# Graph layer with a gathered table: four chunks of edges gathered first as rows of x, all others from the finished table of x W1 and x

## The reference, cut to what matters

```python
theta = x[dst] - x[src]
w = sigmoid(relu(theta @ W1 + b1) @ W2 + b2)
agg = segment_sum(w * theta, dst)
indeg = segment_sum(ones, dst)
y = x + agg + indeg * (x @ W4 + b4)
out = layernorm(y)
```

## Time and profile before

| what | value |
|---|---|
| median of three runs | 4256.39 us |
| the profiled execution | 4260.33 us |
| its span (first to last instruction) | 4258.5 us |
| POOL busy | 3057.1 us (72%) |
| DVE busy | 2904.2 us (68%) |
| PE busy | 1996.0 us (47%), mean granted clock 0.654 |
| ACT busy | 1228.4 us (29%) |
| DMA | 698.18 MB, mean 164 GB/s |

### The profile page before, as it was taken

One profiled execution on the slowest core, in us unless ns is written; L12 is line 12 of the kernel. 1 busy time (PEld: TensorE's weight loads), 2 busy tenths in 40 slices (PEclk: granted clock), 3 DMA queues, 4 the chain that ended last, 5 costly groups with the idle time before them and its releaser, 6 DMA issues.

```text
span 4258.5 us, 43192 instructions
## 1 busy us (share of the span) xinstructions
PE 1996.0 (47%) x10963; PEld 1843.3 (43%) x10963; DVE 2904.2 (68%) x4875; ACT 1228.4 (29%) x2163; POOL 3057.1 (72%) x3229
## 2 busy tenths in 40 slices
PE   3544644444444444444444444444444444444444
PEld 3444644444443444444444444444444444444444
DVE  2332778767777777777777777777777777777777
ACT  2222432322232323322233222232222222222232
POOL 6333677777777777777777777777777777777776
PEclk8776766665666666666666666566666666566666
DMA  5444565555555555555555555555555555555554
GB/s 166 119 125 111 164 177 165 167 172 172 170 168 168 168 168 168 169 169 168 169 169 168 168 168 168 169 169 168 170 171 168 176 165 174 170 169 171 168 168 116
DMA packets 320392, 698.18 MB, mean 164 GB/s; under 512 B 126510, under 2 KB 202496, under 8 KB 305397
## 3 DMA queue, kind: packets, MB, share of 16 engines
q0 software_dynamic: 151344, 408.89, 34.5%
q1 hardware_dynamic: 151920, 262.96, 20.1%
q10 hardware_dynamic: 16879, 23.55, 1.9%
HBM read 663.32 MB, written 31.81 MB: 163 GB/s over the span
## 4 chain that ended last, share of the span: by engine, by line
POOL 63%; issue 21%; PE 5%; DVE 3%; ACTq 3%; DMA 2%; ACT 2%; SPq 1%; POOLq 0%; DVEq 0%
POOL arena L511 63%; ACTq L375 3%; PE ps_z L527 2%; DMA arena<-table,src_at 2%; PE ps_sum L544 1%; SPq L375 1%; DVE scaled_x L691 1%; ACT away L586 1%; ACT hot_ne L594 1%; DVE diff L670 1%; PE ps_z L522 1%; DVE ps_z L661 1%; PE ps_hid L382 1%; DVE logit L678 0%; PE ps_hid L405 0%
## 5 line engine op out<-in xcount | busy, mean ns | idle before, releaser
L511 POOL DMA_INDIRECT arena<-table,src_at x3013 | 2854.9, 948 | 930.8 <-issue 912.7
L544 PE MATMUL ps_sum<-scaled_x,hot_en 128*128 128x130 f32 x6446 | 1395.4, 401 | 1225.7 <-DVE scaled_x L691 1196.1
L544 PEld LDWEIGHTS ps_sum<-scaled_x,hot_en 128*128 128x128 f32 x6446 | 1307.3, 307 | 1289.2 <-issue 1288.3
L661 DVE TENSOR_TENSOR ps_z<-ps_z,arena 128x896 f32<-128x896 f32 x431 | 472.7, 1097 | 906.8 <-DMA arena<-table,src_at 897.6
L601 ACT ACTIVATE ps_log<-logit,b_col 128x7 f32<-128x7 f32 x461 | 124.1, 269 | 2631.5 <-DVE logit L678 2620.1
L691 DVE TENSOR_TENSOR scaled_x<-arena,ps_log 128x896 f32<-128x896 f32 x461 | 496.6, 1077 | 140.1 <-ACT ps_log L601 140.1
L670 DVE SCALAR_TENSOR_TENSOR diff<-ps_z,w_rows 128x896 f32<-128x896 f32 x461 | 502.6, 1090 | 97.2 <-PE ps_z L527 82.4
L678 DVE TENSOR_REDUCE logit<-diff 128x7 f32<-128x896 f32 x461 | 498.1, 1080 | 24.9 <-issue 1.0
L586 ACT ACTIVATE away<-dst_rows,neg_ids 126x896 bf16<-126x896 int32 x461 | 474.3, 1029 | 132.9 <-issue 127.1
L551 PE MATMUL ps_win<-w,winT 128*128 128x256 f32 x232 | 132.4, 671 | 810.8 <-DVE hot_en L683 786.9
L683 DVE TENSOR_TENSOR hot_en<-ps_win,rel 128x896 f32<-128x896 f32 x461 | 497.6, 1079 | 0.0
(11 more groups left out here) (76 smaller groups left out, 824.4 us busy)
## 6 DMA issues: line engine op xcount, KB each, us to landing
dst_rows<-in_dst SPq DMA_DIRECT2D x115, 1764.0 KB
arena<-table,src_at POOLq DMA_INDIRECT x3013
parts<-parts_of SPq DMA_DIRECT2D x461, 31.5 KB
table<-group_rows ACTq DMA_DIRECT2D x25, 500.0 KB
parts_of<-stage SPq DMA_DIRECT2D x116, 96.0 KB, 2.1
winT<-in_x_cols SPq DMA_DIRECT2D x116, 64.0 KB
window<-in_x SPq DMA_DIRECT2D x116, 64.0 KB
out<-yout SPq DMA_DIRECT2D x116, 64.0 KB
```

Source lines behind the costliest of these rows:

```text
L511: nc.gpsimd.indirect_dma_start(gath[:, slot_of(g) + t, :], None, table, ids)\
L544: last = nc.tensor.matmul(ps_sum[:, 0:SW], hot_en[:, b, t, :], scaled_x[:, b, t, :], start=(g == 0 and t == 0), stop=(stop and t == tiles_ ...
L661: v.tensor_tensor(ps_z[b][:, 0:n, :], ps_z[b][:, 0:n, :], gath[:, lo:lo + n, 0:F], ALU.subtract).then_inc(z_read, 1)
```

## The change

POOL now gathers four whole chunks first: chunks 23, 46, 69 and 92 (`z.held`), as rows of x into their own buffer `held_x` (112 gathers). It then waits for the table, for x's half of it and for the checks of the layout, and gathers all other 457 batches (3111 tiles) from the table, in a ring of the same six batches. HEAD and the path of L527 (minus_xT) are gone.

The table is made first, before any batch is computed: the 25 groups run one after the other with five PSUM places. The x half of the table is no longer stored with x W1: SP copies it from x to the table, HBM to HBM, in four transfers of 3125 rows (`copy_x`). ACT loads only the transposed columns and stores only the x W1 half (125 x 4 pieces of 512 bytes per group).

The x W1 of the held chunks (`held_u`) is computed during the 92 batches before each of them, two tiles in four steps on PE and ACT. `dst_rows` is now loaded per batch, by ACT, into three buffers. `diff` has one buffer instead of two. The checks of the layout run at the start.

```diff
-HEAD = 30
+DR = 3
+HC = 4
+STEPS = 4
+BANKS = 5
...
+        self.held = [(h + 1) * self.chunks // (HC + 1) for h in range(HC)]
...
-        dst_rows = sb("dst_rows", [P, 2, CHUNK], I32)
+        held_x = sb("held_x", [P, HC * K, F])
+        held_u = sb("held_u", [P, K, F])
+        held_xT = sb("held_xT", [P, 2, P])
+        dst_rows = sb("dst_rows", [P, DR, BATCH], I32)
...
+        held_chunk = {c: h for h, c in enumerate(z.held)}
+        ringed = [g for g in range(all_batches) if chunk_of(g) not in held_chunk]
...
+            eng.wait_ge(x_copied, 16 * HC)
...
-        def load_group(eng, k):
+        def load_group(act, k):
             s = k % STAGES
-            eng.dma_start(group_rows[0:z.tp, s, :, F:2 * F], in_table(x, k)).then_inc(group_in[s], 16)
-            eng.dma_start(group_cols[:, s, :, :], x_turned[:, k * GT:(k + 1) * GT, :]).then_inc(group_in[s], 16)
+            act.dma_start(group_cols[:, s, :, :], x_turned[:, k * GT:(k + 1) * GT, :]).then_inc(group_in[s], 16)
...
         def copy_group(act, k):
...
+            s = k % STAGES
+            act.wait_ge(turned, k + 1)
+            wait(act, table_out[s], 16 * (k // STAGES))
+            act.sem_inc(act_gate, 1)
+            if k + STAGES < z.groups:
+                load_group(act, k + STAGES)
+            nc.scalar.copy(group_u[0:z.tp, s, :, :], ps_group[k % BANKS][0:z.tp, :, :]).then_inc(turn_copied, 1)
+            act.wait_ge(turn_copied, k + 1)
+            act.dma_start(in_table(table, k)[:, :, 0:F], group_u[0:z.tp, s, :, :]).then_inc(table_out[s], 16)
+
+        def copy_x(sp):
+            each = z.nodes // HC
+            for n in range(HC):
+                sp.dma_start(table[n * each:(n + 1) * each, F:2 * F], x[n * each:(n + 1) * each, :])\
+                    .then_inc(x_copied, 16)
...
         def windows_gpsimd(pool):
...
+            for h, c in enumerate(z.held):
+                if h < 2:
+                    pool.wait_ge(src_in[h], 16 * (h + 1))
+                    pool.sem_inc(pool_gate, 1)
+                for t in range(K):
+                    ids = bass.IndirectOffsetOnAxis(ap=src_at[:, c * K + t:c * K + t + 1], axis=0)
+                    nc.gpsimd.indirect_dma_start(held_x[:, h * K + t, :], None, x, ids).then_inc(held_in[h], 16)
+            wait_for_table(pool)
+            pool.wait_ge(judged, 1)
+            pool.sem_inc(pool_gate, 1)
+            for n, g in enumerate(ringed):
+                if n >= RB:
+                    pool.wait_ge(scaled, ringed[n - RB] + 1)
...
+                if held_step(g):
+                    h, q, step_no = held_step(g)
+                    if step_no == 0:
+                        turn_held(pe, h, q)
+                    if step_no == 2:
+                        project_held(pe, h, q)
```

More of the change, by code:

```diff
@@ L66, in __init__ @@
         self.groups = self.each // GT
-        assert self.groups + 3 <= HEAD < self.batches
+        self.held = [(h + 1) * self.chunks // (HC + 1) for h in range(HC)]
+        assert self.held[0] * NB > K // 2 * STEPS + NB and self.groups > 16
 class Chain:
@@ L394, in copy_group @@
[L394 to L407, removed]
@@ new lines, in turn_held, with copy_heldT @@
+        def turn_held(pe, h, q):
+            pe.wait_ge(held_in[h], 16 * K)
+            pe.wait_ge(turn_copied, z.groups)
+            wait(pe, held_u_copied, h * (K // 2) + q)
+            for t in range(2):
+                last = nc.tensor.transpose(ps_hid[:, t * P:(t + 1) * P], held_x[:, h * K + 2 * q + t, :], ident[:, :])
+            last.then_inc(heldT_ready, 1)
+        def copy_heldT(act, h, q):
+            act.wait_ge(heldT_ready, h * (K // 2) + q + 1)
+            wait(act, held_u_ready, h * (K // 2) + q)
+            nc.scalar.copy(held_xT[:, :, :], ps_hid[:, 0:2 * P].rearrange("p (t e) -> p t e", e=P))\
+                .then_inc(heldT_copied, 1)
@@ new lines, in project_held, with copy_held @@
+        def project_held(pe, h, q):
+            pe.wait_ge(heldT_copied, h * (K // 2) + q + 1)
+            for t in range(2):
+                last = nc.tensor.matmul(ps_hid[:, (2 + t) * P:(3 + t) * P], held_xT[:, t, :], w14[:, 0:F],
+                                        start=True, stop=True)
+            last.then_inc(held_u_ready, 1)
+        def copy_held(act, h, q):
+            act.wait_ge(held_u_ready, h * (K // 2) + q + 1)
+            if h:
+                act.wait_ge(z_read, (z.held[h - 1] + 1) * NB)
+            nc.scalar.copy(held_u[:, 2 * q:2 * q + 2, :], ps_hid[:, 2 * P:4 * P].rearrange("p (t f) -> p t f", f=F))\
+                .then_inc(held_u_copied, 1)
@@ L470, in windows_sync @@
             load_window(sp, 0)
-            load_dst_rows(sp, 0)
-            for k in range(STAGES):
-                load_group(sp, k)
+            copy_x(sp)
             store_parts(sp, 0)
@@ L506, in windows_gpsimd @@
                     ids = bass.IndirectOffsetOnAxis(ap=src_at[:, g * BT + t:g * BT + t + 1], axis=0)
[L507 to L512, removed]
+                    nc.gpsimd.indirect_dma_start(gath[:, slot_of(g) + t, :], None, table, ids)\
+                        .then_inc(gathered[place[g] % RB], 16)
         def windows_tensor(pe):
@@ L613, in mid @@
                 nc.scalar.copy(stage[:, c % 2, 1, :], rest[:, :]).then_inc(mid_ready, 1)
-            high(0)
-            mid(0)
+            for k in range(STAGES):
+                load_group(act, k)
+            for g in range(DR):
+                load_dst_rows(g)
+            for k in range(z.groups):
+                copy_group(act, k)
+                if k == z.groups // 2 + 3:
+                    high(0)
+                if k == z.groups // 2 + 6:
+                    mid(0)
             act.wait_ge(const_in, 16 * 8)
@@ L773, in windows_vector @@
             place_bases(dve)
+            place_rel(dve)
+            select_carry(1)
+            for piece in range(len(JUDGE)):
+                judge(piece)
             dve.wait_ge(const_in, 16 * 8)
```

175 lines of the change are left out of this document (76 added, 99 removed).

## The result

The changed kernel takes 4104.28 us in the median of four runs (4103.46 to 4105.2), against 4257.17 us before (4256.27 to 4260.78): a ratio of 0.9639, 95% interval 0.9623 to 0.9656. That is 3.6% faster; the forecast was 4126 us and 3.1%. The profiled execution has a span of 4103.4 us.

What follows compares the result with a forecast made beforehand. The prediction took POOL, full with gathers from the table, as the bound: first such gather at 212 us + 3111 gathers x 1.252 us (3894.9) + tail 21.1 = 4128 us span, forecast median 4126 us, range 4064 to 4200.

Steps and rivals of the forecast that it cites:

- The bound: Gathers from the table: POOL never waits there, it is simply full.
- period: Time per gather from the table in steady state: kept at 1.252 us, 3111 gathers making 3894.9 us.
- The consumers: Held chunks: consumers take 6.3 to 7.7 us per batch, POOL gathers 3 to 3.5 batches ahead, the six-batch ring suffices.
- Five engines for 3125 rows: Copy of x: engines used are the largest divisor of the row count up to 16, so five of sixteen.
- T0: Start of the first gather from the table: 212 us, from 3.72 MB on each of five engines at 18.6 GB/s.
- rival 2: Copy of x: HBM to HBM pieces cost double, T0 281 us, time 4195 us; chance 14%.
- The floor of T0: Held gathers before the table: 112 x 1.25 us plus 2 x 3 us for held-up gathers, at least 150 us.
- Rival 1: Copy of x is spread or hidden, POOL and ACT set T0 at 150 to 165 us, 4064 to 4079 us; chance 20%.
- The tail: Work behind the last gather: kept at 21.1 us, since its work is the same.
- Sum: Whole span: 212 + 3894.9 + 21.1 = 4128 us.

Runs made afterwards that it cites:

- copy16: The changed kernel with the copy of x in four transfers of 3120 rows and one of 20, over sixteen engines: 4070.07 us, ratio 0.9567 to the kernel before.
- store16: The changed kernel with each group's store split into 112 and 13 partitions, the copy of x still on five engines: 4069.77 us, ratio 0.9565.
- held5: The changed kernel with five held chunks instead of four, the copy of x kept at four transfers: 4067.59 us, ratio 0.9559.
- ring5_again: The changed kernel with a ring of five batches instead of six, repeated on an ordinary chip: 4105.88 us, ratio 0.9643.
- best_third: The changed kernel with five held chunks, stores of 112 and 13 partitions and the bases in PSUM, on an ordinary chip: 4062.35 us, ratio 0.9543.
- held2: The changed kernel with two held chunks instead of four, on a slow chip: 5619.12 us, ratio 0.9954 to the kernel before there.

## Why the prediction was right, and where it was off

- **The bound.** POOL full in steady state, period 1.252: measured 1.2524 after the change. Right. That POOL's gap alone counts was shown three ways (copy16, store16, held5), each worth the 33 us or a little more.
- **The consumers.** The forecast had 3 to 3.5 batches gathered in a held chunk and six in the ring. Measured 27.3 us, 3.1 batches, and ring5_again shows that five suffice. Right. The lag was worked off after some 13 batches of the ring, not 20.
- **Five engines for 3125 rows.** Taken from the counts of three other row numbers, and exact for this one. The Trainium skill's rule (DMA: Bandwidth & Descriptors, on why a DMA increments its semaphore by 16) agrees with 3125, 3120, 20, 112 and 13 rows.
- **T0, 212 us against 181.4: the term that was off.** The load of the five engines was right, their pace of 18.6 GB/s was not. It came from 8.75 us in which one hardware queue and the gathers used them. In the changed kernel, with both queues full, an engine carries in steady state 320 KB of copy in 36.3 us (the median issue of a copy), 67.2 KB of a group in 6.38 us and 4.1 KB of a gather in 1.25 us: 8.8 + 10.5 + 3.3 = 22.6 GB/s. 3.72 MB at this pace is 165 us, and T0 177. The second queue is not the reason: in store16 one hardware queue and the gathers carried 22.2 GB/s on such an engine. So the 8.75 us of the earlier trace rows were a stretch in which the five engines did less than they can, and why they did stays open. The upper bound, a doubled price for a piece from HBM to HBM (rival 2), was not seen: the copy was done by about 170 us.
- **The floor of T0.** Forecast 150 us with 2 x 3 us for held-up gathers; the last held gather ended at 148.1 us and the two took 2.6 and 2.2 us too long. Rival 1 (4064 to 4079 us) described what copy16 then did, with 4070.
- **The tail.** 25.8 instead of 21.1 us. 4.6 us of that lie behind DVE's last instruction (8.4 us to the end of the span, 3.8 before). It varied from 23.4 us (best_third) to 28.9 (ring5_again) in the other versions on ordinary chips; its cause was not looked for.
- **Sum.** -30.6 us (T0) + 1.3 (period) + 4.7 (tail) = -24.6 us against the forecast span of 4128.0, which gives the 4103.4 measured. That period and tail took back 6.0 of the 30.6 us is luck.

## What to carry to other kernels

Where one engine is full from some moment on, write the time as that moment, its instructions times their period, and a tail, and judge an edit by which of the three it moves. Count the packets of a queue to see over how many DMA engines a transfer goes: 125 or 3125 rows use five of sixteen, and a split into a multiple of 16 and a rest costs one more issue. And take an engine's pace from a stretch in which it surely had work all the time, and from more than one: 8.75 us of short transfers gave 18.6 GB/s, 15 us in the middle of a long copy 22.2.

## What the runs showed of the hardware

- The time to issue L397 depended on the store ahead of it on its queue: always the same transfer, it took 5.146 us (median) behind 500 pieces on five shared engines, 2.472 when the copy left them, and 0.358 when the store was split over sixteen and thirteen. Not every transfer held up the next: a store behind L397 was mostly issued in 0.27 us.
- One of the five shared engines moved 22.2 GB/s when one hardware queue and the gathers fed it (store16) and 22.6 when two did (the changed kernel), mostly in pieces of 512 bytes.
- A gather of POOL beside a DVE instruction that reads two operands from SBUF was held until that had ended (3.53 and 3.18 us), and was not with one operand in PSUM (0.94). The Trainium skill says this of GpSimd instructions that read SBUF (SBUF — State Buffer, on what contends for the shared ports); each gather reads its column of indices there, but that this read is what has to wait is not shown.
- The kernel before took 4254 to 4257 us on some chips and 5638 or 5667 us on two others. There POOL was no longer the bound: DVE waited 1772.1 us in L707 (held2), and what ended these waits was PE's increment.
